# Second cross attention of a decoder megakernel: residual and normalisation of a pair moved from VectorE to ScalarE and GpSimd

## The chip, the cores and the metric

The kernel runs on one core of one Trainium2 chip. The metric is device time in microseconds of one launch, shown as the median of three runs. TensorE is called PE below, VectorE DVE, ScalarE ACT, GpSimd Pool, and SyncE (which issues the loads) SP.

## The reference

Two decoder layers with post-normalisation over 32 sequences of 56 tokens, width 128, with a context of 32 x 1500 x 128. Each layer runs attention, cross attention and a mixture of experts; the change is in the cross attention of the second layer:

```python
    def _L1_xattn_ref(x, context, ln_gamma, ln_beta, w_q, w_kv, w_out, b_out, gate):
        ...
        xn = _layernorm(x, ln_gamma, ln_beta)
        q = (xn @ w_q).reshape(B, SQ, NUM_HEADS, DIM_HEAD)
        kv = context @ w_kv
        ...
        scores = jnp.einsum('bqhd,bkhd->bhqk', q * SCALE, k)
        attn = jax.nn.softmax(scores, axis=-1)
        out = jnp.einsum('bhqk,bhkd->bqhd', attn, v).reshape(B, SQ, INNER)
        out = out @ w_out + b_out
        return out * jnp.tanh(gate[0])
...
    x = _layernorm(x + _L1_xattn_ref(x, ctx_1024, L1_xattn_ln_gamma, ...), axis=-1)
```

The outer `_layernorm` in the last line subtracts the mean over the 128 features and divides by the square root of variance plus 1e-5. It and the sum `x + ...` are what the change concerns.

## The kernel before, in words

The whole decoder is one program of phases. The phase of the change, `state_cross_phase`, works on 16 pairs of sequences (2 x 56 tokens, padded to 128 rows). For each pair there are 14 units of work (`NU`), each with 128 rows (8 queries times 16 heads) of scores against 1500 context positions. The engines' programs are written by hand as a software pipeline: `run` calls `step(i, s)` for pair `i` and slot `s` from 0 to 13; pair 0 is written out (`first`), pairs 1 to 14 are a hardware loop of 14 turns, pair 15 is written out (`end`), then comes an epilogue. Order on an engine is the order of the code; engines meet at semaphores, and every queue is in order.

In slot `s` of pair `i`:

- PE computes the scores of unit `s` (`scores`, nine matmuls of 500 columns in three pieces of three; a piece waits until the bank has been freed by DVE's `low_part` of unit `s - 2`), then one part of the value product of an older group (`values`, L2098 to L2100), then whatever the slot tables add.
- DVE inverts the sum of unit `s - 1` (`inverse`, L2226, L2228), takes the maximum of unit `s` (`maximum`, L2217 needs the first two pieces of the scores, L2221 the third), then writes the low half of the probabilities of unit `s - 1` (`low_part`, L2237, three parts).
- ACT takes the exponential of unit `s` once the maximum is there (`exponentials`, L2426, L2429, with the sum by accumulation), and writes the high half of unit `s` (`high_part`, L2445) once DVE has the inverse.
- SP issues the transposing DMA of unit `s`, and in slot 8, behind that, the load of the next pair's second context half, `load_T(i + 1, 1)` (L1807), into the only buffer `ctxT`.
- Pool prepares the next operands in 16-bit halves (`split_q`, `split_c`, `split_n`) and multiplies each context half with its scale when it has landed: `scale_c(i + 1, 1)` (L1939, 128x1500) is the last of a turn.

The output of pair `i - 1` is finished beside pair `i`. PE's output product `y` (L2133) is made in slots 7, 8 and 9 (`OUTPUT`). In slot 10 (`RESIDUAL`) DVE makes `r = gate * y + xg` between `inverse` and `maximum`, and its mean and variance (`vector_moments`, L265 and L269). Pool's `xg` (L1912) is `x` plus the gated bias; Pool adds epsilon (L274) and takes the power -1/2 (L279). In slot 11 (`NORMALISE`) DVE writes the normalised `xn` (L296) behind its `low_part`. In slot 12 (`STORE`) PE transposes `xn` (L336) behind its `values`, and ACT keeps the transposed tile (L345, L353) between its exponential and its `high_part`. In slot 13 (`LOGITS`) PE makes the router's logits (L359) from it. Pool copies `xn` back to `x_tok` (L330).

Of the kernel before, what the change touches and what calls it, by code (L numbers as in the profile page):

```python
# [28 lines left out]
PAIRS = B // 2  # L29
# [1621 lines left out]
def state_cross_phase(k):  # L1651
# [19 lines left out]
    FIRST_BANKS = (0, 1, 2, 3)  # L1671
    PROJECT, OUTPUT, RESIDUAL, NORMALISE, STORE, LOGITS = {2: 0, 3: 1, 4: 2, 5: 3}, {7: 0, 8: 1, 9: 2}, 10, 11, 12, 13
    OUTPUT_HEADS = (0, 6, 11, H1)
# [9 lines left out]
    with ExitStack() as ctx:  # L1683
# [50 lines left out]
        on = sb("on", [128, H1, 2, SP])  # L1734
        gated_bias, xg = sb("gated_bias", [128, D]), sb("xg", [128, 1, D])
        psum = ctx.enter_context(nc.psum_tensor("xa_psum", [128, 8, 512], fp32))
# [14 lines left out]
        pv_ready, on_kept = sem("pv_ready"), sem("on_kept")  # L1751
        on_zeroed, y_ready, bias_ready, xg_ready = sem("on_zeroed"), sem("y_ready"), sem("bias_ready"), sem("xg_ready")
        two_ready = sem("two_ready")
        flat_psum = psum[:, :, :].rearrange("p a b -> p (a b)")
# [107 lines left out]
        def _(pool):  # L1862
            open_sems(pool, 2, c_hi_ready, c_lo_ready, c_scaled, n_scaled, n_hi_ready, n_lo_ready, q_hi_ready, q_lo_ready)
            t.open_pool(pool)
            open_sems(pool, 1, xg_ready)

# [102 lines left out]
            def windows(i, first=False, end=False):  # L1969
                split_q(i, 1)  # L1970
                split_c(i, 1)
                split_n(i, 0, first)
                if not end:
                    scale_c(i + 1, 0)
                    split_q(i + 1, 0)
                    split_c(i + 1, 0)
                split_n(i, 1)
                if not first:
                    gated(i - 1)
                    t.pool_rstd(pool, i - 1, 0)  # L1980
                    t.pool_store(pool, i - 1, 0)
                if not end:
                    scale_c(i + 1, 1)

            for c in range(NB):
# [12 lines left out]
            gated(PAIRS - 1)  # L1998
            t.pool_rstd(pool, PAIRS - 1, 0)
            t.pool_store(pool, PAIRS - 1, 0)  # L2000

        @block.tensor
        def _(pe):
# [100 lines left out]
            def turn(i, u, r, first=False, end=False):  # L2104
# [85 lines left out]
            def epilogue():  # L2190
# [6 lines left out]
                for part in range(len(OUTPUT)):  # L2197
                    outputs(i, part)
                pe.wait_ge(t.r_ready, this(i))
                t.tensor_transpose(pe, i, 0, psum[:, 7, 128:256])  # L2200
# [6 lines left out]
        def _(dve):  # L2207
            open_sems(dve, NU, two_ready, max_ready, total_ready, rinv_ready)
            open_sems(dve, NL * NU, h2_ready)
            open_sems(dve, NR, *turn_kept.values())  # L2210
            t.open_vector(dve)

# [58 lines left out]

# [104 lines left out]
            def epilogue():  # L2376
                i = PAIRS - 1
                inverse(i, NU - 1)
                keep_turned(i, TURNED[1], 0)
                low_part(i, NU - 1)  # L2380
                keep_turned(i, TURNED[1], 1)
                keep_turned(i, TURNED[1], 2)
                residual(i)
                t.vector_normalise(dve, i, 0)
                t.vector_logits(dve, i, 0, psum[:, 7, 0:E])
# [4 lines left out]
        def _(act):  # L2390
            open_sems(act, NB, q_kept)
            open_sems(act, NU, exp_ready, bias_scaled)
            open_sems(act, 2 * NU, h1_ready)
            open_sems(act, NG, on_kept)
            t.open_scalar(act)

            def evacuate(i, g):
# [332 lines left out]
```

## Time and profile before

| | |
|---|---|
| median of 3 runs | 1885.1 us (1882.76 to 1885.45) |
| the profiled execution, its own time | 1884.88 us |
| its span, first to last instruction | 1883.0 us |
| busy over the span: PE, DVE, ACT, Pool | 1667.1, 1549.9, 1275.3, 925.5 us |
| mean granted TensorE clock | 0.96 |

A busy share is an average over phases with different limits, and PE's matmul spans overlap each other in the records (a matmul of 500 columns is shown with 0.37 us, and the next starts 0.21 us later), so the shares do not say which engine sets the pace. The phase of the change runs from about 600 to 1706 us. Within it the 14 turns of the loop repeat each other to within a few hundredths of a microsecond every 67.5 us, so that one turn read closely stands for all.

### The profile page before, as it was taken

The page shows a single profiled execution, that of the slowest core. Times are in us where ns is not written, and L with a number is a line of the kernel's source. Part 1 is how long each engine was busy: PE and PEld are TensorE (multiplying, and loading weights), DVE is VectorE, ACT ScalarE, POOL GpSimd, SP SyncE. Part 2 cuts the span into 40 slices and gives each one's busy share as a digit, 9 for nine tenths or more (in the row PEclk, how much of TensorE's full clock was granted, in tenths as well). Part 3 has the DMA queues.
Part 4 walks back from the last instruction along what each step waited for, and adds up shares of the span by engine and source line. Part 5 has one row for each costly group of instructions (what it writes and reads, how often), then busy time and mean ns, then how long its engine had stood idle before and what let it go on. Part 6 is the DMA issues. An engine that isn't in the chain of part 4 may idle for free. (4 is left out here: it accounts for less than half of the span.)

```text
span 1883.0 us, 34675 instructions
## 1 busy us (share of the span) xinstructions
PE 1667.1 (89%) x10425; PEld 1009.4 (54%) x10425; DVE 1549.9 (82%) x2885; ACT 1275.3 (68%) x2106; POOL 925.5 (49%) x723
## 2 busy tenths in 40 slices
PE   4987996889957899999999999999999999994997
PEld 2654665777733344554554554454455455454886
DVE  2765785877758999999999999999999999975887
ACT  2442332877735887887888788788788888864554
POOL 3640111363335766565665656656567465421333
PEclk9997998799978999999999999999999999997998
DMA  5203884311100898988899898898888889973231
GB/s 190 95 0 127 306 332 173 85 42 45 45 34 17 180 197 174 199 182 179 190 183 190 183 190 187 178 195 182 179 199 179 188 183 185 182 135 122 47 79 29
DMA packets 632266, 281.85 MB, mean 150 GB/s; under 512 B 601852, under 2 KB 606236, under 8 KB 631452
## 3 DMA queue, kind: packets, MB, share of 16 engines
q1 hardware_dynamic: 632204, 281.10, 64.2%
q8 instruction: 30, 0.49, 0.1%
q14 instruction: 32, 0.26, 0.0%
HBM read 129.02 MB, written 1.05 MB: 69 GB/s over the span
## 5 line engine op out<-in xcount | busy, mean ns | idle before, releaser
L2237 DVE SCALAR_TENSOR_TENSOR xa_h<-xa_psum,xa_rinv,xa_h 128x500 f16<-128x500 f32 x672 | 452.8, 730 | 1.0 <-ACT xa_h L2445 0.7
L2445 ACT ACTIVATE xa_h<-xa_psum,xa_rinv 128x1000 f16<-128x1000 f32 x448 | 371.5, 883 | 51.8 <-DVE xa_rinv L2228 51.5
L2429 ACT ACTIVATE xa_psum<-xa_psum,xa_bias,unscale_s 128x1500 f32<-128x1500 f32 x224 | 353.2, 1577 | 7.4
L2073 PE MATMUL xa_psum<-xa_c_hi,xa_q_hi 128*128 128x500 f16 x672 | 257.4, 383 | 54.5 <-DVE xa_h L2237 50.1
L2217 DVE TENSOR_REDUCE xa_psum<-xa_psum 128x1 f32<-128x1000 f32 x224 | 269.3, 1202 | 14.2 <-PE xa_psum L2075 13.4
L2098 PE MATMUL xa_psum<-xa_prT,xa_n_hi 128*128 128x512 f16 (+1 forms) x768 | 270.8, 353 | 3.6 <-issue 1.6
L2100 PE MATMUL xa_psum<-xa_prT,xa_n_lo 128*128 128x512 f16 (+1 forms) x768 | 270.6, 352 | 0.0
L2099 PE MATMUL xa_psum<-xa_prT,xa_n_hi 128*128 128x512 f16 (+1 forms) x768 | 270.6, 352 | 0.0
L2074 PE MATMUL xa_psum<-xa_c_lo,xa_q_hi 128*128 128x500 f16 x672 | 252.7, 376 | 0.0
L2075 PE MATMUL xa_psum<-xa_c_hi,xa_q_lo 128*128 128x500 f16 x672 | 252.4, 376 | 0.0
L1939 POOL TENSOR_SCALAR xa_ctxT<-xa_ctxT,scales 128x1500 f32<-128x1500 f32 x31 | 126.3, 4073 | 166.4 <-DMA xa_ctxT<-in_ctxT 166.4
L2221 DVE TENSOR_REDUCE xa_negmax<-xa_psum 128x1 f32<-128x512 f32 x224 | 154.9, 692 | 25.7
L2073 PEld LDWEIGHTS xa_psum<-xa_c_hi,xa_q_hi 128*128 128x128 f16 x672 | 65.0, 97 | 199.2 <-DVE xa_h L2237 177.7
L1463 DVE TENSOR_TENSOR moe_hid_lo<-moe_hid,moe_hid_hi 128x448 fp32r<-128x448 f32 x200 | 129.9, 675 | 34.3 <-ACT moe_hid_hi L1614 28.7
L2426 ACT ACTIVATE xa_bias<-xa_negmax,unscale_s 128x1 f32<-128x1 f32 x224 | 66.9, 299 | 134.5 <-DVE xa_negmax L2221 128.2
L1960 POOL TENSOR_SCALAR xa_ctxP<-xa_ctxP,scales 128x1536 f32<-128x1536 f32 x32 | 133.5, 4171 | 19.7 <-DMA xa_ctxP<-in_ctxP 19.7
L2098 PEld LDWEIGHTS xa_psum<-xa_prT,xa_n_hi 128*128 128x128 f16 x768 | 76.1, 99 | 92.1 <-issue 16.8
L1310 POOL TENSOR_TENSOR moe_acc<-moe_acc,moe_part 128x448 f32<-128x448 f32 x52 | 64.3, 1236 | 105.4 <-DVE moe_part L1539 53.9
L2100 PEld LDWEIGHTS xa_psum<-xa_prT,xa_n_lo 128*128 128x128 f16 x768 | 75.0, 98 | 70.2
L1610 ACT ACTIVATE moe_hid<-moe_psum,up_bias 128x448 f32<-128x448 f32 x128 | 84.2, 658 | 38.8 <-PE moe_psum L1372 34.3
L2099 PEld LDWEIGHTS xa_psum<-xa_prT,xa_n_hi 128*128 128x128 f16 x768 | 75.0, 98 | 65.2
L2075 PEld LDWEIGHTS xa_psum<-xa_c_hi,xa_q_lo 128*128 128x128 f16 x672 | 65.9, 98 | 77.5 <-issue 1.8
(328 smaller groups left out, 3630.4 us busy)
## 6 DMA issues: line engine op xcount, KB each, us to landing
ctxN<-in_ctxP SPq DMA_DIRECT2D x16, 1536.0 KB, 9.5
xa_ctxP<-in_ctxP SPq DMA_DIRECT2D x32, 768.0 KB, 4.3
ctxT<-in_ctxT SPq DMA_DIRECT2D x16, 1500.0 KB, 6.4
xa_ctxT<-in_ctxT SPq DMA_DIRECT2D x32, 750.0 KB, 4.7
moe_spread<-weight_rows SPq DMA_DIRECT2D x16, 1024.0 KB, 8.4
xa_prT<-xa_h SPq DMA_TRANSPOSE x192, 5.5
up<-in_F_up SPq DMA_DIRECT2D x1, 2048.0 KB, 7.7
down<-in_F_down SPq DMA_DIRECT2D x1, 2048.0 KB, 11.8
```

What stands on the lines that cost most here:

```text
L1960: pool.tensor_scalar(ctxP[:, :], ctxP[:, :], k.scales[:, 0:1], None, ALU.mult).then_inc(n_scaled, 1)
L2073: nc.tensor.matmul(out, qh, c_hi[:, b, a:z], start=True, stop=False)
L2074: nc.tensor.matmul(out, qh, c_lo[:, b, a:z], start=False, stop=False)
L2075: done = nc.tensor.matmul(out, ql, c_hi[:, b, a:z], start=False, stop=True)
L2098: nc.tensor.matmul(out, nh, ph, start=(kt == 0), stop=False)
L2099: nc.tensor.matmul(out, nh, pl, start=False, stop=False)
L2100: done = nc.tensor.matmul(out, nl, ph, start=False, stop=(kt == KT - 1))
L2217: nc.vector.tensor_reduce(psum[:, bank + 1, W:W + 1], psum[:, bank:bank + 2, 0:W], AX.XY, ALU.max)\
L2221: nc.vector.tensor_reduce(negmax[:, s % 2, :], flat_psum[:, top:top + 512], AX.X, ALU.max, negate=True)\
L2237: nc.vector.scalar_tensor_tensor(low, psum[:, bank + a:bank + z, 0:W], rinv[:, s % 2, :], high, ALU.mult, ALU.subtract).then_inc(h2_ready, 1)
L2429: nc.scalar.activation(psum[:, bank:bank + 3, 0:W], psum[:, bank:bank + 3, 0:W], ACT.Exp, bias=bias[:, s % 2, :], scale=k.unscale_s[:, :], ...
L2445: nc.scalar.activation(h[:, H_SLOT[s], 0, a * W:z * W].rearrange("p (a c) -> p a c", c=W), psum[:, bank + a:bank + z, 0:W], ACT.Identity, ...
```

## The change

VectorE no longer has the residual, the moments and the normalisation of a pair. ACT and Pool make them, in another arithmetic: the sum of `xg` (ACT, slot 7, `sum_x`) and the sum of the gated `y` (ACT, slot 9, `gate`, which also writes the gated `y` to the new tile `yg`) come by accumulation; Pool adds `r = yg + xg` and makes minus the mean (`residual`); ACT squares `r` minus the mean with the sum by accumulation (slot 11, `square`); Pool makes variance plus epsilon, the power, `xn`, and its copy (`normalise`). `gated` is earlier in Pool's turn. PE, where it waited for `r_ready` before it overwrote the bank of `y`, waits for `yg_ready`. The two moments differ from those of `bn_stats` in rounding alone.

```diff
@@ gpsimd @@
             def gated(i):
                 pool.wait_ge(bias_ready, 1)
                 pool.wait_ge(t.r_ready, last(i))
+                pool.sem_inc(gating, 1)
+                pool.wait_ge(x_sum_ready, last(i))
                 pool.tensor_tensor(xg[:, :, :], k.x_tok[:, bass.ds(i, 1), :], gated_bias[:, :].unsqueeze(1), ALU.add)\
                     .then_inc(xg_ready, 1)
+
+            def residual(i):
+
+                pool.wait_ge(yg_ready, this(i))
...
+                pool.tensor_tensor(t.r[:, :, :], yg[:, :, :], xg[:, :, :], ALU.add).then_inc(t.r_ready, 1)
+                pool.wait_ge(x_sum_ready, this(i))
+                pool.sem_inc(gating, 1)
+                pool.tensor_scalar(neg_mean[:, :], y_sum[:, :], x_sum[:, :], -1.0 / D, ALU.add, ALU.mult)\
+                    .then_inc(neg_mean_ready, 1)
+
+            def normalise(i):
+
+                pool.wait_ge(squares_ready, this(i))
...
+                pool.tensor_scalar(t.var_eps[:, 0, :], squares[:, :], 1.0 / D, k.eps[:, :], ALU.mult, ALU.add)\
+                    .then_inc(t.var_eps_ready, 1)
...
+                pool.tensor_tensor(t.rstd[:, 0, :], t.var_eps[:, 0, :], k.minus_half[:, :], ALU.pow).then_inc(t.rstd_ready, 1)
...
+                pool.tensor_scalar(t.xn[:, 0, :], t.r[:, 0, :], neg_mean[:, :], t.rstd[:, 0, :], ALU.add, ALU.mult)\
+                    .then_inc(t.xn_ready, 1)
+                t.pool_store(pool, i, 0)
...
                 split_n(i, 0, first)
+                if not first:
+                    gated(i - 1)
                 if not end:
                     scale_c(i + 1, 0)
                     split_q(i + 1, 0)
                     split_c(i + 1, 0)
                 split_n(i, 1)
                 if not first:
-                    gated(i - 1)
-                    t.pool_rstd(pool, i - 1, 0)
-                    t.pool_store(pool, i - 1, 0)
+                    residual(i - 1)
                 if not end:
                     scale_c(i + 1, 1)
+                if not first:
+                    normalise(i - 1)
@@ tensor @@
                 if u == TURNED[0] and r == 1 and not first:
-                    pe.wait_ge(t.r_ready, this(i - 1))
+                    pe.wait_ge(yg_ready, this(i - 1))
@@ vector @@
-            def residual(i):
-
-                dve.wait_ge(y_ready, this(i))
-                dve.wait_ge(xg_ready, this(i))
-                nc.vector.scalar_tensor_tensor(t.r[:, 0, :], psum[:, 7, 0:128], k.gate_tanh[:, :], xg[:, 0, :],
-                                               ALU.mult, ALU.add).then_inc(t.r_ready, 1)
-                t.vector_moments(dve, i, 0)
...
-                if s == RESIDUAL and not first:
-                    residual(i - 1)
...
-                if not first:
-                    if s == NORMALISE:
-                        t.vector_normalise(dve, i - 1, 0)
@@ scalar @@
+            def sum_x(i):
...
+                nc.scalar.activation(yg[:, 0, :], xg[:, 0, :], ACT.Identity, accum_out=x_sum[:, :]).then_inc(x_sum_ready, 1)
+
+            def gate(i):
+
+                act.wait_ge(y_ready, this(i))
+                act.wait_ge(x_sum_ready, this(i))
+                nc.scalar.activation(yg[:, 0, :], psum[:, 7, 0:128], ACT.Identity, scale=k.gate_tanh[:, :],
+                                     accum_out=y_sum[:, :]).then_inc(yg_ready, 1)
+
+            def square(i):
+
+                act.wait_ge(t.r_ready, this(i))
+                act.wait_ge(neg_mean_ready, this(i))
+                act.wait_ge(t.var_eps_ready, last(i))
+                nc.scalar.activation(yg[:, 0, :], t.r[:, 0, :], ACT.Square, bias=neg_mean[:, :],
+                                     accum_out=squares[:, :]).then_inc(squares_ready, 1)
...
             def step(i, s, first=False, end=False):
                 exponentials(i, s)
+                if s == min(OUTPUT) and not first:
+                    sum_x(i - 1)
+                if s == max(OUTPUT) and not first:
+                    gate(i - 1)
+                if s == SQUARES and not first:
+                    square(i - 1)
                 if s == STORE and not first:
                     t.scalar_store(act, i - 1, 0, psum[:, 7, 128:256])
```

Where the instructions stand. First DVE, slot 10 of a loop turn, before the change; line 2217 is the first half of `maximum`:

```order
704 L2228 RECIPROCAL xa_rinv<-xa_total 128x1
705 L2249 REGISTER_ALU
706 L2251 SCALAR_TENSOR_TENSOR xa_r<-xa_psum,gate_tanh,xa_xg 128x128
707 L265 BN_STATS xa_moments<-xa_r 128x6
708 L269 BN_AGGR xa_mean_var<-xa_moments 128x2
709 L2216 REGISTER_ALU
710 L2217 TENSOR_REDUCE xa_psum<-xa_psum 128x1
```

With the change nothing stands between the two in that slot (`maximum` is line 2260 there, the reciprocal 2271):

```order
704 L2271 RECIPROCAL xa_rinv<-xa_total 128x1
705 L2259 REGISTER_ALU
706 L2260 TENSOR_REDUCE xa_psum<-xa_psum 128x1
```

Three instructions before a `maximum` are gone from DVE, and the one of slot 11 (L296) too.

Second Pool, the end of a loop turn, before the change; the branch is the loop's end:

```order
339 L1967 TENSOR_TENSOR xa_n_lo<-xa_ctxP,xa_n_hi 128x1536
340 L1912 ISA
341 L1912 TENSOR_TENSOR xa_xg<-x_tok,xa_gated_bias 128x128
342 L274 TENSOR_TENSOR xa_var_eps<-xa_mean_var,eps 128x1
343 L279 TENSOR_TENSOR xa_rstd<-xa_var_eps,minus_half 128x1
344 L330 COPY x_tok<-xa_xn 128x128
345 L1937 REGISTER_ALU
346 L1939 TENSOR_SCALAR xa_ctxT<-xa_ctxT,scales 128x1500
347 L1995 REGISTER_ALU
348 L1995 COMPARE_AND_BRANCH
```

The same place with the change:

```order
341 L2008 TENSOR_TENSOR xa_n_lo<-xa_ctxP,xa_n_hi 128x1536
342 L1928 TENSOR_TENSOR xa_r<-xa_yg,xa_xg 128x128
343 L1931 TENSOR_SCALAR xa_neg_mean<-xa_y_sum,xa_x_sum 128x1
344 L1978 REGISTER_ALU
345 L1980 TENSOR_SCALAR xa_ctxT<-xa_ctxT,scales 128x1500
346 L1940 TENSOR_SCALAR xa_var_eps<-xa_squares,eps 128x1
347 L1945 TENSOR_TENSOR xa_rstd<-xa_var_eps,minus_half 128x1
348 L1952 TENSOR_SCALAR xa_xn<-xa_r,xa_neg_mean,xa_rstd 128x128
349 L330 COPY x_tok<-xa_xn 128x128
350 L2038 REGISTER_ALU
```

The scaling of the context (128x1500) stood behind the pair's tail; it now stands ahead of variance, power and `xn`.

Third ACT in slots 12 and 13 of the changed kernel, where the order itself did not change (L345 waits for PE's transposition of `xn`):

```order
621 L2480 ACTIVATE xa_psum,xa_rs<-xa_psum,xa_bias,unscale_s 128x3x500
622 L345 ACTIVATE xa_xnT<-xa_psum 128x128
623 L353 ISA
624 L353 ACTIVATE x_feat<-xa_psum 128x112
625 L2496 ACTIVATE xa_h<-xa_psum,xa_rinv 128x1000
```

The store still stands between exponential and high half, so ACT too waits there if `xn` is late.

## Rows read from the trace of the kernel before

**Rows 1.** Windows: busy time (and count) of each engine, clock, DMA share, GB/s

```profile
core 0: us, PE busy (x) PEld busy (x) DVE busy (x) ACT busy (x) POOL busy (x), PEclk, DMA share, GB/s
1285.00:1350.00 65.00, 62.14 (x391) 32.48 (x388) 59.97 (x105) 53.99 (x82) 38.94 (x21) 1.00 0.90 189
```

**Rows 2.** Timeline of DVE: start, duration, line; idle before and its releaser

```profile
1253.54 1.21 DVE L2217 TENSOR_REDUCE xa_psum<-xa_psum 128x1 f32<-128x1000 f32 x1 [0.48 <-PE xa_psum L2075]
...
1258.02 0.35 DVE L2251 SCALAR_TENSOR_TENSOR xa_r<-xa_psum,gate_tanh,xa_xg 128x128 f32<-128x128 f32 x1
...
1258.85 0.18 DVE L269 BATCH_NORM_AGGREGATE xa_mean_var<-xa_moments 128x2 f32<-128x6 f32 x1 [0.15 <-DVE xa_moments L265]
1259.08 1.21 DVE L2217 TENSOR_REDUCE xa_psum<-xa_psum 128x1 f32<-128x1000 f32 x1
...
1267.96 0.34 DVE L296 TENSOR_SCALAR xa_xn<-xa_r,xa_mean_var,xa_rstd 128x128 f32<-128x128 f32 x1
...
1273.49 1.21 DVE L2217 TENSOR_REDUCE xa_psum<-xa_psum 128x1 f32<-128x1000 f32 x1
...
1703.17 0.35 DVE L296 TENSOR_SCALAR xa_xn<-xa_r,xa_mean_var,xa_rstd 128x128 f32<-128x128 f32 x1 [0.93 <-POOL xa_rstd L279]
```

**Rows 3.** Timeline of PE: sixth score matmuls, starts after a wait, the transposition

```profile
1253.13 0.37 PE L2075 MATMUL xa_psum<-xa_c_hi,xa_q_lo 128*128 128x500 f16 x1
...
1258.09 0.37 PE L2075 MATMUL xa_psum<-xa_c_hi,xa_q_lo 128*128 128x500 f16 x1
...
1261.81 0.38 PE L2073 MATMUL xa_psum<-xa_c_hi,xa_q_hi 128*128 128x500 f16 x1 [0.32 <-DVE xa_h L2237]
...
1270.69 0.27 PE L336 MATMUL xa_psum<-ident,xa_xn 128*128 128x128 f32 x1
1271.82 0.39 PE L2073 MATMUL xa_psum<-xa_c_hi,xa_q_hi 128*128 128x500 f16 x1 [0.85 <-DVE xa_h L2237]
...
1272.89 0.37 PE L2075 MATMUL xa_psum<-xa_c_hi,xa_q_lo 128*128 128x500 f16 x1
...
1703.66 0.42 PE L336 MATMUL xa_psum<-ident,xa_xn 128*128 128x128 f32 x1 [2.47 <-DVE xa_xn L296]
```

**Rows 4.** Instructions of line 2251: count, durations, first and last start

```profile
L2251 DVE SCALAR_TENSOR_TENSOR xa_r<-xa_psum,gate_tanh,xa_xg x16: 350/351/352, 717.7 to 1701.2; 128x128 f32<-128x128 f32 x16
```

**Rows 5.** Timeline of ACT in slots 9 to 12

```profile
1258.11 1.66 ACT L2445 ACTIVATE xa_h<-xa_psum,xa_rinv 128x1000 f16<-128x1000 f32 x2 [0.48 <-DVE xa_rinv L2228]
...
1267.97 0.19 ACT L2429 ACTIVATION_READ_ACCUMULATOR xa_psum<-xa_psum,xa_bias,unscale_s 128x1 f32 x1
...
1273.08 0.27 ACT L345 ACTIVATE xa_xnT<-xa_psum 128x128 f32<-128x128 f32 x1
```

**Rows 6.** Timeline of Pool

```profile
1233.99 4.07 POOL L1939 TENSOR_SCALAR xa_ctxT<-xa_ctxT,scales 128x1500 f32<-128x1500 f32 x1 [11.08 <-DMA xa_ctxT<-in_ctxT]
...
1259.11 0.19 POOL L274 TENSOR_TENSOR xa_var_eps<-xa_mean_var,eps 128x1 f32<-128x1 f32 x1 [2.66 <-DVE xa_mean_var L269]
1259.38 0.57 POOL L279 TENSOR_TENSOR xa_rstd<-xa_var_eps,minus_half 128x1 f32<-128x1 f32 x1
...
1268.74 4.08 POOL L1939 TENSOR_SCALAR xa_ctxT<-xa_ctxT,scales 128x1500 f32<-128x1500 f32 x1
```

**Rows 7.** Timeline of SP: issues of the two context loads of a turn

```profile
1229.06 0.35 SPq L1807 DMA_DIRECT2D xa_ctxT<-in_ctxT  x1
...
1261.66 0.34 SPq L1807 DMA_DIRECT2D xa_ctxT<-in_ctxT  x1
```

**Rows 8.** Groups of Pool's instructions, whole span: busy us, mean ns

```profile
L1287 POOL TENSOR_SCALAR key_query<-key_query,scales 128x512 f32<-128x512 f32 x4 | 9.6, 2392 | 0.0
...
L1912 POOL TENSOR_TENSOR xa_xg<-x_tok,xa_gated_bias 128x128 f32<-128x128 f32 x16 | 7.3, 458 | 0.0
...
L1875 POOL TENSOR_SCALAR ss_spread_inner<-ss_mean_var 128x4 f32<-128x4 f32 x4 | 2.9, 720 | 12.6 <-DVE ss_mean_var L2320 12.5
...
L1900 POOL TENSOR_SCALAR xa_gated_bias<-bout_row1x,gate_tanh 128x128 f32<-128x128 f32 x1 | 0.6, 618 | 0.0
```

More of the change, by code:

```diff
@@ L1671, in state_cross_phase @@
     FIRST_BANKS = (0, 1, 2, 3)
-    PROJECT, OUTPUT, RESIDUAL, NORMALISE, STORE, LOGITS = {2: 0, 3: 1, 4: 2, 5: 3}, {7: 0, 8: 1, 9: 2}, 10, 11, 12, 13
+    PROJECT, OUTPUT, SQUARES, STORE, LOGITS = {2: 0, 3: 1, 4: 2, 5: 3}, {7: 0, 8: 1, 9: 2}, 11, 12, 13
     OUTPUT_HEADS = (0, 6, 11, H1)
@@ L1734, in state_cross_phase @@
         on = sb("on", [128, H1, 2, SP])
-        gated_bias, xg = sb("gated_bias", [128, D]), sb("xg", [128, 1, D])
+        gated_bias, xg, yg = sb("gated_bias", [128, D]), sb("xg", [128, 1, D]), sb("yg", [128, 1, D])
+        y_sum, x_sum, neg_mean, squares = (sb(n, [128, 1]) for n in ("y_sum", "x_sum", "neg_mean", "squares"))
         psum = ctx.enter_context(nc.psum_tensor("xa_psum", [128, 8, 512], fp32))
@@ L1752, in state_cross_phase @@
         on_zeroed, y_ready, bias_ready, xg_ready = sem("on_zeroed"), sem("y_ready"), sem("bias_ready"), sem("xg_ready")
+        yg_ready, x_sum_ready, sum_ready = sem("yg_ready"), sem("x_sum_ready"), sem("sum_ready")
+        neg_mean_ready, squares_ready, gating = sem("neg_mean_ready"), sem("squares_ready"), sem("gating")
         two_ready = sem("two_ready")
@@ L1864, in _ @@
             t.open_pool(pool)
+            open_sems(pool, 1, t.r_ready, t.xn_ready, neg_mean_ready)
             open_sems(pool, 1, xg_ready)
@@ L1911, in gated @@
                 pool.wait_ge(t.r_ready, last(i))
+                pool.sem_inc(gating, 1)
+                pool.wait_ge(x_sum_ready, last(i))
                 pool.tensor_tensor(xg[:, :, :], k.x_tok[:, bass.ds(i, 1), :], gated_bias[:, :].unsqueeze(1), ALU.add)\
                     .then_inc(xg_ready, 1)
+            def residual(i):
+                pool.wait_ge(yg_ready, this(i))
+                pool.sem_inc(gating, 1)
+                pool.wait_ge(squares_ready, last(i))
+                pool.sem_inc(gating, 1)
+                pool.wait_ge(t.xn_ready, last(i))
+                pool.tensor_tensor(t.r[:, :, :], yg[:, :, :], xg[:, :, :], ALU.add).then_inc(t.r_ready, 1)
+                pool.wait_ge(x_sum_ready, this(i))
+                pool.sem_inc(gating, 1)
+                pool.tensor_scalar(neg_mean[:, :], y_sum[:, :], x_sum[:, :], -1.0 / D, ALU.add, ALU.mult)\
+                    .then_inc(neg_mean_ready, 1)
+            def normalise(i):
+                pool.wait_ge(squares_ready, this(i))
+                pool.sem_inc(gating, 1)
+                pool.wait_ge(t.rstd_ready, last(i))
+                pool.sem_inc(gating, 1)
+                pool.tensor_scalar(t.var_eps[:, 0, :], squares[:, :], 1.0 / D, k.eps[:, :], ALU.mult, ALU.add)\
+                    .then_inc(t.var_eps_ready, 1)
+                pool.wait_ge(t.var_eps_ready, this(i))
+                pool.sem_inc(gating, 1)
+                pool.wait_ge(t.xn_ready, last(i))
+                pool.tensor_tensor(t.rstd[:, 0, :], t.var_eps[:, 0, :], k.minus_half[:, :], ALU.pow).then_inc(t.rstd_ready, 1)
+                pool.wait_ge(t.rstd_ready, this(i))
+                pool.sem_inc(gating, 1)
+                pool.wait_ge(t.xnT_ready, last(i))
+                pool.sem_inc(gating, 1)
+                pool.wait_ge(t.tok_stored, last(i))
+                pool.sem_inc(gating, 1)
+                pool.tensor_scalar(t.xn[:, 0, :], t.r[:, 0, :], neg_mean[:, :], t.rstd[:, 0, :], ALU.add, ALU.mult)\
+                    .then_inc(t.xn_ready, 1)
+                t.pool_store(pool, i, 0)
             def split_q(i, b):
@@ L1998, in _ @@
             gated(PAIRS - 1)
-            t.pool_rstd(pool, PAIRS - 1, 0)
-            t.pool_store(pool, PAIRS - 1, 0)
+            residual(PAIRS - 1)
+            normalise(PAIRS - 1)
         @block.tensor
@@ L2198, in epilogue @@
                     outputs(i, part)
-                pe.wait_ge(t.r_ready, this(i))
+                pe.wait_ge(yg_ready, this(i))
                 t.tensor_transpose(pe, i, 0, psum[:, 7, 128:256])
@@ L2210, in _ @@
             open_sems(dve, NR, *turn_kept.values())
-            t.open_vector(dve)
+            open_sems(dve, 1, t.logits_kept)
             def maximum(i, s):
@@ L2382, in epilogue @@
                 keep_turned(i, TURNED[1], 2)
-                residual(i)
-                t.vector_normalise(dve, i, 0)
                 t.vector_logits(dve, i, 0, psum[:, 7, 0:E])
@@ L2394, in _ @@
             open_sems(act, NG, on_kept)
+            open_sems(act, 1, x_sum_ready, yg_ready, squares_ready)
             t.open_scalar(act)
+            def sum_x(i):
+                act.wait_ge(xg_ready, this(i))
+                act.wait_ge(squares_ready, last(i))
+                act.wait_ge(neg_mean_ready, last(i))
+                nc.scalar.activation(yg[:, 0, :], xg[:, 0, :], ACT.Identity, accum_out=x_sum[:, :]).then_inc(x_sum_ready, 1)
[10 more added lines that the diff above has]
+                                     accum_out=squares[:, :]).then_inc(squares_ready, 1)
             def evacuate(i, g):
@@ L2515, in epilogue @@
                         evacuate(*at)
+                sum_x(PAIRS - 1)
+                gate(PAIRS - 1)
+                square(PAIRS - 1)
                 t.scalar_store(act, PAIRS - 1, 0, psum[:, 7, 128:256])
```

## The prediction, made blind

> **What bounds the kernel now.** Windows first. A stretch of about one loop turn has PE busy 62.1 of 65 us, DVE 60.0, ACT 54.0, Pool 38.9, at full clock [rows 1]. PE and DVE are both near full, so the shares decide nothing; the order of waits inside a turn does. The timelines give it, read at one turn; its 14 copies start 67.5 us apart.
>
> In most slots DVE sets the pace: inverse, maximum, low half, with PE waiting for the low half to free a bank, as in slot 11 at 1261.81 after 0.32 us idle and in slot 13 at 1271.82 after 0.85 us [rows 3]. Slots 8 to 10 are different, since PE also makes the output product there: the maximum of slot 9 starts at 1253.54 after 0.48 us idle, released by PE [rows 2]. Its sixth score matmul started at 1253.13 [rows 3], so a maximum can start 0.41 us after the sixth matmul's start. That rule prices everything below.
>
> **What goes from DVE.** In slot 10 the residual, the statistics and the aggregation stand between 1258.02 and 1259.08, when the maximum starts [rows 2]: 1.06 us on DVE's path. But PE's sixth matmul of that slot started at 1258.09 [rows 3], so without them the maximum waits for PE until 1258.50. The gain is 0.58 us, not 1.06. It survives slot 11 nearly whole: PE had 0.32 us of idle there and would start at 1261.49; its sixth matmul at 1.07 more (1271.82 to 1272.89 is the same distance [rows 3]) allows the maximum at 1262.97, about where DVE, 0.58 us early, asks for it. I take 0.55. The `xn` of slot 11, at 1267.96 for 0.34 us [rows 2], ends at 1268.30, 0.14 us after ACT's accumulator read of the same slot (1267.97 + 0.19 = 1268.16 [rows 5]), which the next inverse needs anyway: removing it is worth 0.1 us at most, and I take nothing.
>
> **What ACT gets.** Three activations of 128x128 with a sum: 0.27 us for such a tile and 0.19 for the accumulator read [rows 5], about 0.45 each. They follow the exponentials of slots 7, 9 and 11, where ACT otherwise waits for DVE's inverse, 0.48 us in slot 9 [rows 5]. That wait hides them; if it were gone they would cost 0.45 us each, up to 1.4 per turn. Dearer ones (0.65) would still push only a high half, which DVE needs after the whole maximum. Cost taken: nothing. The gated `y` is there at about 1258.0, and the turned-tile matmuls of PE that wait for it come after slot 10's values, so that wait costs nothing either.
>
> **What Pool gets, and where it lands.** Here I expect the time to go. Before, Pool made variance and power at 1259.11 and 1259.38 (0.19 and 0.57 us), waited for DVE's `xn`, and only then scaled the context, at 1268.74 for 4.08 us [rows 6]. Now `scale_c` stands ahead of variance, power and `xn`. It can't run early: its data's load is issued by SP in slot 8, behind a transposing DMA, at 1261.66 [rows 7], and nothing of the change moves slot 8. Landing: the other load of the turn was issued at 1229.06 [rows 7] and Pool, which was waiting for it, started at 1233.99 [rows 6], 4.93 us later. I take 4.85: `scale_c` runs from 1266.5 to 1270.6. The squares are there by about 1268.1, so Pool's queue, not ACT, holds the tail back.
>
> Then the three operations on Pool. Variance: a tensor_scalar of one column, not in this trace; below by the add of 0.19 us [rows 6], above by the 128x4 with two operations, 0.72 us [rows 8]; I take 0.4, between them, as it is a quarter as wide. Power: 0.57 [rows 6]. `xn`: a tensor_scalar of 128x128 with two operations; below by the add of that size, 0.46, nearer by the one with one operation, 0.62 [rows 8]; above by 2.39 us for 512 columns [rows 8], which scaled by size and doubled for two operations gives 1.2; I take 0.8. Two gaps of 0.08 (1259.11 + 0.19 to 1259.38 [rows 6]). Sum N = 0.4 + 0.57 + 0.8 + 0.16 = 1.93, bounds 1.38 and 2.65. So `xn` is there at 1270.57 + 1.93 = 1272.50, where it was at 1268.30.
>
> PE transposed at 1270.69, without a wait [rows 3], and would be there by 1270.15 now. It must wait for `xn`. After a late `xn`, in the epilogue, the matmul started 0.14 us after its end (1703.17 + 0.35 [rows 2] to 1703.66 [rows 3]). So transposition at 1272.64, the scores of slot 13 queued behind it at about 1272.8, their sixth matmul 1.07 later, the maximum at 1274.28. It was 1273.49 [rows 2]. The 0.55 us of slot 10 are lost and 0.79 us more. ACT, which waits in slot 12 for the transposed tile before its high half, has it at 1272.9 and is done before DVE's low half asks; the logits come later than both. Nothing gives the time back: PE and DVE shift alike.
>
> In sentences of its own: the Trainium skill, page GPSIMD Engine Reference, section Engine selection, says that one-input elementwise work on Pool runs at roughly line rate, and its cycle accounting gives about 1.03 cycles an element for it. By that, `xn` would be some 0.3 us (an estimate from that page) and a pair would lose about 0.1 us. Here the trace disagrees: 1500 columns of a one-input multiplication took 4.07 us [rows 6], 2.7 ns each, so I stay with the rows.
>
> **The sum.** 14 turns hold `scale_c` ahead of the tail: 14 x 0.79 = +11.1 us. Pair 15's steps have no such load and keep the gain: -0.5. The epilogue is serial: from the residual's start at 1701.2 [rows 4] to `xn`'s end at 1703.52 [rows 2] was 2.3 us. Now: gate 0.45, `r` 0.46, minus mean 0.4, square 0.45, variance 0.4, power 0.57, `xn` 0.8, and six hand-overs of 0.08 make 4.0: +1.7. Together +12.3. The profiled execution took 1884.9 (span 1883.0), the median is 1885.1; the forecast is 1897.
>
> Bounds: with N = 1.38 a turn loses 0.24, with cheap Pool work the epilogue +1.1: +4.0, 1889. With N = 2.65, 1.51 a turn and +3 at the end: +23.6, 1908.
>
> **The rivals.** Faster (0.11): Pool's tail does not hold PE. Point of decision: a turn wins if the maximum of slot 13 starts before 1273.49, so `xn` must be there by 1271.7. This needs the load landed 0.8 us sooner than its twin, or N below 1.14, under my lower bound. For it: the gain of slot 10 is certain, and PE has 0.85 us of slack before slot 13. If the tail were wholly hidden: 14 x -0.55 - 0.5 + 1.7 = -6.5, 1878.5.
>
> About no change (0.09): the Pool operations cost what the cheapest rows say, or the page's rule holds, and the loss of a turn is 0.0 to 0.25 us. That gives 1885 to 1889. Against it: no tensor_scalar in the rows is as cheap as an add.
>
> Slower by another way (0.05): PE's idle stretch of 2.5 us a turn makes the granted clock fall from 2.4 to 1.2 GHz. In the rows it stayed at 1.00 with 0.85 us of idle per turn [rows 1, 3]. If slot 13's nine score matmuls then ran at half speed, 9 x 0.21 = 1.9 us a turn, +27 more: 1924. Slower by ACT, with its three extras on the path, would be 14 x 1.4 less the gain: 1897 also, told apart by where DVE waits. The forecast itself has 0.75.
>
> **Numbers.** Range 1884 to 1908: the forecast with its bounds and the no-change case; the faster case and the clock stay out. Within 0.2% (3.8 us, about what a measurement of this kernel can tell): 0.10, faster 0.11, slower 0.79.
>
> **What the profile after would show.** No DVE instruction between reciprocal and maximum in slot 10, the maximum starting 0.4 us after PE's sixth matmul. `scale_c` of the second half starting on a DMA wait, about 4.9 us after its issue, ending some 2 us before `xn`. PE idle over 2 us before L336, released by Pool's `xn`, once a turn; DVE idle 1.4 us before slot 13's maximum, released by PE. A loop turn of 68.3 us. I am wrong if L336 has no wait, if Pool runs the small operations in under 1.2 us together, if the load lands before 1265.5 in this turn's time, or if ACT's idle before its bias is used up in slots 7, 9 or 11.

## The result, and the profile after

Before: 1883.4 us median of 6 runs (1881.3 to 1885.5). After: 1901.1 us median of 6 runs (1896.9 to 1907.8). The ratio is 1.0097 with a 95% interval of 1.0078 to 1.0116: slower by some 17.6 us, where 12 were forecast. The profiled execution of after is the slowest of its six, 1907.8 us with a span of 1905.9, against 1884.9 and 1883.0 before; what follows must explain 22.9 us in this one execution and 17.6 in the median, and the two are not the same.

First the page of after, its busy times and two of its groups (busy us, mean ns, then idle time just before and what ended it):

```profile
PE 1671.2 (88%) x10425; PEld 1018.8 (53%) x10425; DVE 1536.6 (81%) x2821; ACT 1289.8 (68%) x2202; POOL 944.9 (50%) x771
...
L2260 DVE TENSOR_REDUCE xa_psum<-xa_psum 128x1 f32<-128x1000 f32 x224 | 269.3, 1202 | 47.7 <-PE xa_psum L2118 47.6
...
L1980 POOL TENSOR_SCALAR xa_ctxT<-xa_ctxT,scales 128x1500 f32<-128x1500 f32 x31 | 126.1, 4067 | 267.9 <-DMA xa_ctxT<-in_ctxT 267.9
```

The maximum (L2260, the L2217 of before) sat idle for 14.2 us in the whole program before, nearly all of it for PE; now it is 47.7. The waits between the start of the first pair's loop turn and the last one's, in after, grouped by who waited and for what (total us, count, longest):

```profile
DVE xa_psum L2260 <- PE xa_psum L2118: 43.0, 59, 3.3
...
PE xa_psum L336 <- POOL xa_xn L1952: 33.8, 14, 3.0
```

Fourteen waits of PE for Pool's `xn` are one per turn, 2.4 us each (1.9 to 3.0). Before, the transposition started in the loop without a wait [rows 3]. The timeline of Pool in the turn that the prediction followed, now 1265 to 1282 (start, duration, line, operation; idle before it and its releaser):

```profile
1266.24 0.45 POOL L1928 TENSOR_TENSOR xa_r<-xa_yg,xa_xg 128x128 f32<-128x128 f32 x1 [2.22 <-ACT xa_yg L2437]
1266.67 0.27 POOL L1931 TENSOR_SCALAR xa_neg_mean<-xa_y_sum,xa_x_sum 128x1 f32<-128x1 f32 x1
1274.38 4.07 POOL L1980 TENSOR_SCALAR xa_ctxT<-xa_ctxT,scales 128x1500 f32<-128x1500 f32 x1 [7.44 <-DMA xa_ctxT<-in_ctxT]
1278.44 0.26 POOL L1940 TENSOR_SCALAR xa_var_eps<-xa_squares,eps 128x1 f32<-128x1 f32 x1
1278.89 0.57 POOL L1945 TENSOR_TENSOR xa_rstd<-xa_var_eps,minus_half 128x1 f32<-128x1 f32 x1 [0.18 <-POOL xa_var_eps L1940]
1279.87 0.44 POOL L1952 TENSOR_SCALAR xa_xn<-xa_r,xa_neg_mean,xa_rstd 128x128 f32<-128x128 f32 x1 [0.41 <-POOL xa_rstd L1945]
```

Pool stands idle for 7.44 us for the load, with the tail queued behind the scaling, and the tail's input long there: ACT's accumulator read of the squares started at 1275.76 and took 0.19. The load's issue on SP:

```profile
1265.67 3.66 SPq L1833 DMA_TRANSPOSE xa_prT<-xa_h  x1
1269.67 0.34 SPq L1810 DMA_DIRECT2D xa_ctxT<-in_ctxT  x1
```

From 1269.67 to 1274.38 are 4.71 us. PE and DVE in the same turn, PE first:

```profile
1277.94 0.33 PE L2143 MATMUL xa_psum<-xa_prT,xa_n_lo 128*128 128x384 f16 x1
1280.45 0.30 PE L336 MATMUL xa_psum<-ident,xa_xn 128*128 128x128 f32 x1 [2.19 <-POOL xa_xn L1952]
1280.59 0.37 PE L2116 MATMUL xa_psum<-xa_c_hi,xa_q_hi 128*128 128x500 f16 x1
1281.64 0.37 PE L2118 MATMUL xa_psum<-xa_c_hi,xa_q_lo 128*128 128x500 f16 x1
```

```profile
1265.84 0.16 DVE L2271 RECIPROCAL xa_rinv<-xa_total 128x1 f32<-128x1 f32 x1
1266.49 1.21 DVE L2260 TENSOR_REDUCE xa_psum<-xa_psum 128x1 f32<-128x1000 f32 x1 [0.49 <-PE xa_psum L2118]
...
1280.78 0.16 DVE L2271 RECIPROCAL xa_rinv<-xa_total 128x1 f32<-128x1 f32 x1
1282.06 1.21 DVE L2260 TENSOR_REDUCE xa_psum<-xa_psum 128x1 f32<-128x1000 f32 x1 [1.11 <-PE xa_psum L2118]
```

In slot 10 (first two rows) nothing is left between reciprocal and maximum but 0.49 us of waiting for PE: the time from slot 9's maximum to this one went from 5.53 to 4.96 us, 0.57 less. In slot 13 (last two) DVE waits 1.11 us for PE, whose scores stand behind the transposition: the time from slot 12's maximum to slot 13's went from 4.39 us to 5.25 at the least.

That is what was forecast. The lengths of the 14 loop turns (start of the maximum of slot 0 to the next one's) show what was not:

| | turns, us | sum |
|---|---|---|
| before | 67.5 each | 945.4 |
| after, forecast | 68.3 each | 956.5 |
| after, 7 turns | 67.85 to 68.45, mean 68.12 | 476.9 |
| after, the other 7 | 69.32 to 70.39, mean 69.83 | 488.8 |

The long ones are 1.7 us longer than the short ones. Two things are in that. Their load came later: PE's wait for `xn` has a mean of 2.7 us in them and 2.15 in the short ones, 0.5 us of the 1.7. In each of the seven short turns the length is 65.97 or 65.98 us plus that wait, so a wait longer by some time makes the turn longer by the same time. The long turns hold 1.0 to 1.4 us beyond that sum, 1.2 on average. These 1.2 are here, in the windows of one of them, with the granted clock behind the busy times of PE, PEld, DVE, ACT and Pool:

```profile
1345.00:1348.00 3.00, 1.43 (x9) 0.65 (x7) 2.87 (x5) 2.13 (x4) 2.82 (x3) 1.00 1.03 196
1348.00:1350.00 2.00, 0.93 (x3) 0.55 (x4) 0.93 (x3) 1.18 (x5) 0.81 (x3) 0.61 0.95 186
1350.00:1352.00 2.00, 2.00 (x6) 0.73 (x5) 0.00 (x0) 1.54 (x2) 0.00 (x0) 0.54 0.78 310
1352.00:1354.00 2.00, 2.00 (x14) 1.30 (x13) 1.84 (x3) 0.00 (x0) 1.11 (x2) 1.00 0.00 0
```

PE is busy without a break up to 1346.43 (the 1.43 us of the first window), then idle for 2.64, and comes back to a clock at half, 1.2 GHz instead of 2.4, until six of the nine score matmuls are through. Its timeline there:

```profile
1349.07 0.45 PE L336 MATMUL xa_psum<-ident,xa_xn 128*128 128x128 f32 x1 [2.64 <-POOL xa_xn L1952]
1349.31 0.63 PE L2116 MATMUL xa_psum<-xa_c_hi,xa_q_hi 128*128 128x500 f16 x1
1349.73 0.62 PE L2117 MATMUL xa_psum<-xa_c_lo,xa_q_hi 128*128 128x500 f16 x1
...
1351.39 0.61 PE L2118 MATMUL xa_psum<-xa_c_hi,xa_q_lo 128*128 128x500 f16 x1
```

0.61 instead of 0.37, and a maximum that starts 2.97 us after the transposition instead of 1.61. Such a fall is in each of the seven long turns and in no short one. The moment differs: in this turn the clock is at half 0.63 us before PE works again, in others only when PE has worked for up to 1.1 us. So this execution's loop holds 7 x 0.6 + 7 x 2.3 = +20.3 us. Pair 15 and the epilogue (last slot-0 maximum to the start of PE's transposition of `xn`) went from 87.65 to 89.15, +1.5. Together +21.8 of the 22.9; the rest lies behind that transposition, in phases that the change leaves alone.

### The profile page after: what moved, and what is told of

The parts are those of the page before. It is cut to its first block and busy times, and to the rows that moved or that the text cites. A ratio compares the mean times of both kernels' runs of the same rounds, so it can differ in the third digit from the quotient of the medians.

```text
span 1905.9 us, 34885 instructions
## 1 busy us (share of the span) xinstructions
PE 1671.2 (88%) x10425; PEld 1018.8 (53%) x10425; DVE 1536.6 (81%) x2821; ACT 1289.8 (68%) x2202; POOL 944.9 (50%) x771
## 5 line engine op out<-in xcount | busy, mean ns | idle before, releaser
L2260 DVE TENSOR_REDUCE xa_psum<-xa_psum 128x1 f32<-128x1000 f32 x224 | 269.3, 1202 | 47.7 <-PE xa_psum L2118 47.6
```

The costliest lines, as they stand in the source:

```text
L2260: nc.vector.tensor_reduce(psum[:, bank + 1, W:W + 1], psum[:, bank:bank + 2, 0:W], AX.XY, ALU.max)\
```

## The experiments

Theory A, after the result: Pool's order. The tail stands behind a scaling that waits for a load, `xn` is late for PE, and the late `xn` costs a turn directly (0.6 to 0.8 us) and, when the clock falls in PE's idle stretch, over a microsecond more. Theory B: the operations added to ACT and Pool, or the removed ones of DVE, are dear wherever they stand. Theory C: the lost time is all clock. The times before in each pair below are of the same chip in the same hours.

**e1_tail_first.** One call of Pool's order is moved, so that the tail stands ahead of the load-bound scaling:

```diff
                 if not first:
                     residual(i - 1)
+                    normalise(i - 1)
...
                 scale_c(i + 1, 1)
-                if not first:
-                    normalise(i - 1)
```

> The changed kernel with Pool's normalise put back ahead of scale_c of the second context half; ACT's and DVE's parts are as changed. Theory (the tail is late because it stands behind scale_c, which waits for its load): xn is ready about 1.9 us after the squares, before PE reaches its transposition or at most a few tenths after, PE's wait before L336 goes from 2.2 us and more to under 0.3 us, no turn shows half clock, a loop turn takes 67.0 us (67.5 before, less the 0.57 us of slot 10), and the time is 14 x 0.57 + 0.3 = 8.3 below before, plus 1.7 for the epilogue: about 1877, ratio 0.9965. Rival A (Pool's arithmetic itself is too slow, wherever it stands): L336 still waits over 1 us, 1890 or more. Rival B (ACT's three extra activations are on the path): slots 8, 10 and 12 get longer by some 0.4 us each, over 1895.

Measured: 1879.2 us, median of 12 runs, against 1884.2 before: ratio 0.9972 [0.9961, 0.9983]. All arithmetic of the change is in it, and it is faster than before (1877 was expected). Pool and PE in its timeline:

```profile
1266.31 0.27 POOL L1940 TENSOR_SCALAR xa_var_eps<-xa_squares,eps 128x1 f32<-128x1 f32 x1 [9.32 <-ACT xa_yg L2444]
1267.74 0.45 POOL L1952 TENSOR_SCALAR xa_xn<-xa_r,xa_neg_mean,xa_rstd 128x128 f32<-128x128 f32 x1 [0.41 <-POOL xa_rstd L1945]
1268.63 4.08 POOL L1980 TENSOR_SCALAR xa_ctxT<-xa_ctxT,scales 128x1500 f32<-128x1500 f32 x1
```

```profile
1268.33 0.30 PE L336 MATMUL xa_psum<-ident,xa_xn 128*128 128x128 f32 x1
1269.26 0.38 PE L2115 MATMUL xa_psum<-xa_c_hi,xa_q_hi 128*128 128x500 f16 x1 [0.63 <-DVE xa_h L2279]
```

The tail runs before the load has landed, `xn` is there at 1268.2, and PE transposes without a wait. The 14 turns last 66.98 us on average (673.17 to 1610.83), all at full clock. Measured from maximum to maximum, this turn differs from before in two slots alone: 0.58 us less up to slot 10's and 0.12 more from slot 13's to the next slot 0's, of which more below; every other slot is within 0.01. So neither ACT's three activations nor the missing `xn` of DVE shows in the turn. Theory B falls; the scaling, put behind the tail, starts without any wait and is late for nobody.

**e3_load_slot7.** Pool's order stays as in after, and the load is issued a slot earlier:

```diff
-                if s == 8 and not end:
+                if s == 7 and not end:
                     load_T(i + 1, 1)
```

> The changed kernel with one number different: SP issues the load of the second context half in slot 7, not 8, and Pool's order is as changed (scale_c ahead of the tail). Theory: the load lands 4.9 us sooner, scale_c ends at about 1265.7 of the turn shown, before the squares are there, so the tail is as early as with the order undone: about 1877, turns of 67.0 us, full clock. Rival (it is the place in the queue as such, not the landing): no better than 1897. If the earlier load delays the transposing DMAs behind it, values of PE start late in slots 11 and 12, and the gain is smaller by that wait.

Measured: 1879.4 us, median of 12, ratio 0.9976 [0.9964, 0.9987]; turns of 66.98 us. The issue on SP, then Pool:

```profile
1252.18 0.34 SPq L1810 DMA_DIRECT2D xa_ctxT<-in_ctxT  x1
```

```profile
1257.39 4.07 POOL L1980 TENSOR_SCALAR xa_ctxT<-xa_ctxT,scales 128x1500 f32<-128x1500 f32 x1 [3.05 <-DMA xa_ctxT<-in_ctxT]
...
1263.66 0.27 POOL L1940 TENSOR_SCALAR xa_var_eps<-xa_squares,eps 128x1 f32<-128x1 f32 x1 [2.20 <-ACT xa_yg L2445]
```

Now the tail waits for ACT and no longer for the load. Two edits that share nothing but the tail no longer waiting for the load give the same turn within 0.01 us: the place is found.

**e4_before_swapped.** The kernel before, with all its work on DVE, and only Pool's order spoiled in the same way:

```diff
-                    t.pool_rstd(pool, i - 1, 0)
-                    t.pool_store(pool, i - 1, 0)
...
                 scale_c(i + 1, 1)
+                if not first:
+                    t.pool_rstd(pool, i - 1, 0)
+                    t.pool_store(pool, i - 1, 0)
```

> The kernel before, with nothing moved between engines, only scale_c of the second half put ahead of Pool's variance and power (pool_rstd) and store. Theory: the power is ready only when scale_c has ended, 4.07 us after a landing at 1266.4 of the turn shown: 1271.3 with 0.85 us of variance and power; DVE stands in its queue with xn from 1267.95 on, so it stalls some 3.3 us and everything behind it: +3.3 x 14 = +46, 1930. This is worse than the change (0.6 to 2.8 us a turn), since there only PE, with 0.85 us of slack, stands and waits. Rival (the order matters little and the change's loss is in its arithmetic): within 5 us of before.

Measured: 1945.9 us, median of 4, ratio 1.0328 [1.0311, 1.0346]: +62, the largest number of the study, with none of the change in it. In its timeline Pool first, then DVE, where the normalisation stands in the middle of the queue and holds every maximum behind it:

```profile
1300.78 4.07 POOL L1939 TENSOR_SCALAR xa_ctxT<-xa_ctxT,scales 128x1500 f32<-128x1500 f32 x1 [9.68 <-DMA xa_ctxT<-in_ctxT]
1305.08 0.57 POOL L279 TENSOR_TENSOR xa_rstd<-xa_var_eps,minus_half 128x1 f32<-128x1 f32 x1
```

```profile
1305.68 0.34 DVE L296 TENSOR_SCALAR xa_xn<-xa_r,xa_mean_var,xa_rstd 128x128 f32<-128x128 f32 x1 [3.02 <-POOL xa_rstd L279]
```

The slot takes 8.1 to 8.6 us instead of 5.0, the 3.3 that I expected; but a turn is 4.4 us longer (the 14 take 61.4 more), and the other 1.1 us, 15 in all, I had not in my number. Windows there (the clock is the first figure behind the five busy times):

```profile
1306.00:1310.00 4.00, 0.78 (x4) 0.35 (x4) 3.84 (x8) 2.75 (x4) 0.29 (x1) 1.00 0.96 266
1310.00:1314.00 4.00, 4.00 (x16) 1.93 (x15) 3.69 (x9) 3.57 (x8) 1.51 (x2) 0.62 0.06 23
```

PE is busy 0.78 of 4 us, and the clock is at half behind it; such a fall is in all 14 turns. The 1.1 us lie in the two slots behind the stall, in which the clock is at half (0.9 to 2.2 us by turn); all slots ahead of it last as long as before. So a direct loss and one with the clock are here also. PE's idle time around the transposition is 1.49 us ahead of it and 2.25 behind it in this turn, more together than in after, and here no turn was spared.

**e2_filled and e5_filled_loop.** To part the clock from the late `xn`: after, with matmuls whose result nobody reads put into PE's wait, 18 of 256 columns, in a bank's unused half. e2 has them in all of pairs 1 to 15, e5 leaves them out in pair 15. The edit of e5:

```diff
+                    for x in range(0 if end else FILL):
+                        nc.tensor.matmul(psum[:, 7, 256:512], k.kq_hi[:, 0, :],
+                                         k.kq_hi[:, 0:2, :], start=True, stop=True)
                     t.tensor_transpose(pe, i - 1, 0, psum[:, 7, 128:256])
```

> The changed kernel with 18 matmuls of 256 columns of a constant tile, whose result nobody reads, on PE in slot 12 just before its wait for xn (1.9 us of work in a stretch in which PE is idle for 2.2 us and more). Theory (two separate losses: the late xn itself, about 0.6 us a turn against before, and half clock after the idle stretch, about 1.3 to 2.3 us in those turns in which it falls): all 14 turns look like the fast ones of the profile after, 67.9 to 68.5 us, no half clock in the loop, 14 x 0.6 + 1.5 = 10 above before, about +1 for pair 15, where nothing waits and the filling is in the way: 1893 to 1895, some 6 us below the changed kernel. Rival (the slow turns are slow because of DMA or Pool, and the clock is only a mark of them): the spread of turns stays, time as with the change, 1901.

> As the filled kernel before, but the 18 filling matmuls stand only in the turns in which scale_c is ahead of the tail (pairs 1 to 14), not in pair 15, where they cost 1.0 us. Compared on one chip with the changed kernel itself. Theory (the idle stretch of PE costs a clock fall in some turns, a loss of its own): no turn at half clock, turns of 67.8 to 68.7 us by how late the load lands, 14 x 0.7 + 1.5 = 11 to 13 above before, and below the changed kernel by 1.7 us for each of its turns at half clock. Rival (the clock falls are harmless here): equal to the changed kernel within 0.1%.

Measured: e2 1900.0, median of 6, ratio 1.0084 [1.0068, 1.0101]; e5 1899.2, median of 6, ratio 1.0067 [1.0053, 1.0081]. PE's timeline in e5:

```profile
1277.64 2.13 PE L2204 MATMUL xa_psum<-kq_hi 128*128 128x256 f16 x18
1280.33 0.33 PE L336 MATMUL xa_psum<-ident,xa_xn 128*128 128x128 f32 x1 [0.56 <-POOL xa_xn L1953]
```

PE is idle 0.56 us instead of 2.2, no loop turn of either shows a clock below 1.00, and none is longer than 69.0 us: e5's 14 last 956.5 us together, 68.3 each, which is the forecast's sum. Theory C falls, since most of the loss stays. But e2 had been expected at 1893 to 1895, 6 us under after, as I had taken seven long turns for typical; it is only 1 us under after's median. Its own loop, +10.4 us on before, is as expected; its last stretch is 2.8 us longer than before, since the filling is in the way of pair 15, and in its profile the loop starts 2 us later than before's (in all the profiles here it starts between 667.8 and 673.2 us). That asked for after a second time.

**e6_after_again.** After, unchanged, on the same chip as e5.

> The changed kernel once more, unaltered, for the comparison on one chip and a second profile. Theory: ratio 1.0097 as measured; the turns fall in two groups again, 67.8 to 68.6 us at full clock and 69 to 70.5 at half clock, in another number than the 7 of the first profile, since which turns fall is not fixed by the program; the time of the profiled execution moves by some 1.7 us for each. Rival (the slow turns belong to fixed pairs): the same turns are slow.

Measured: 1902.2 us, median of 4, ratio 1.0093 [1.0077, 1.0109], against e5's 1899.2. Its profiled execution is its fastest, 1897.5, and there only one turn of 14 has the half clock. The windows in that turn:

```profile
1612.00:1618.00 6.00, 3.62 (x21) 1.71 (x19) 5.54 (x11) 4.87 (x9) 5.24 (x5) 1.00 1.04 210
1618.00:1622.00 4.00, 4.00 (x16) 2.12 (x17) 2.44 (x6) 2.28 (x5) 1.16 (x2) 0.66 0.62 204
```

Its other 13 turns have a mean of 68.3 us, each 65.95 or 65.96 plus PE's wait; the 14 are 957.5 together, +12.1 on before. It is the last turn that has the half clock, and six others that had it in the first profile have not. So how many turns the clock spoils is not fixed by the program: 7 in one execution of after, 1 in another, with nearly the same idle before the transposition (37.5 us in all before L336, 38.2 in after's). Nor is it a matter of the idle's length alone: in after's profile the clock fell behind an idle of 2.12 us in one turn and not behind 2.48 in another, and e6 has one of 2.88 without a fall. The two profiled executions are the slowest (1907.8) and the fastest but one (1897.5) of ten; their loops are 8.2 us apart, and six more falls of 1.2 make 7.2 of that.

**e7_epilogue_dve.** e1, and the last pair's residual, statistics and normalisation made by DVE again, in the epilogue alone. Not shown in the cut: ACT's three activations of the last pair go, and PE waits for `r_ready` there.

```diff
 # DVE, epilogue
+                residual(i)
+                t.vector_normalise(dve, i, 0)
 # Pool, epilogue
-            residual(PAIRS - 1)
-            normalise(PAIRS - 1)
+            t.pool_rstd(pool, PAIRS - 1, 0)
+            t.pool_store(pool, PAIRS - 1, 0)
 # DVE, start of the phase
+            open_sems(dve, PAIRS, t.moments_ready, t.mean_var_ready)
```

> The kernel with Pool's tail ahead of scale_c, and in the epilogue, where the chain is serial and DVE idle, the last pair's residual, moments and normalisation on DVE as before the change. Theory: from the residual's start to xn's end 2.3 us again instead of 4.2, so 1.9 us below that kernel's profile and about 7.5 below before: ratio 0.9961, the fastest of all. Rival (the epilogue is hidden by loads or table loads of the next phase): no difference to the kernel with the order undone.

Measured: 1876.4 us, median of 6, ratio 0.9953 [0.9939, 0.9967], the fastest version of the study. The last stretch went from e1's 89.2 to 87.3, as expected. Its timeline of DVE in the epilogue:

```profile
1688.62 0.35 DVE L2294 SCALAR_TENSOR_TENSOR xa_r<-xa_psum,gate_tanh,xa_xg 128x128 f32<-128x128 f32 x1 [14.54 <-PE xa_psum L2175]
...
1690.57 0.34 DVE L296 TENSOR_SCALAR xa_xn<-xa_r,xa_mean_var,xa_rstd 128x128 f32<-128x128 f32 x1 [0.94 <-POOL xa_rstd L279]
```

2.3 us from the residual's start to `xn`'s end, as before, where ACT and Pool take 4.2 (from the start of ACT's `gate`). But its loop turns were 66.86 us, and not e1's 66.98, and no edit of e7 is in the loop. In e1 the reciprocal of slot 0 stood so on DVE (e1's timeline):

```profile
1275.23 0.16 DVE L2270 RECIPROCAL xa_rinv<-xa_total 128x1 f32<-128x1 f32 x1
1275.46 0.69 DVE L2285 COPY xa_prT<-xa_psum 128x1024 f16<-128x1024 f16 x1
```

and in e7's:

```profile
1268.81 0.17 DVE L2271 RECIPROCAL xa_rinv<-xa_total 128x1 f32<-128x1 f32 x1
1268.91 0.69 DVE L2286 COPY xa_prT<-xa_psum 128x1024 f16<-128x1024 f16 x1
```

From one start to the next 0.23 us there, 0.10 here. Before had 0.11.

**e8_two_more and e9_tail_first_again.** e8 is e1 with only the last edit of e7: two semaphores more, raised once at the start of the phase on DVE, at 549.7 us, over 700 us ahead of these rows, and waited for by nobody. e9 is e1 again, on e8's chip.

> The kernel with Pool's tail ahead of scale_c, and two more semaphore increments in DVE's program ahead of its first work (of two semaphores nobody waits for); nothing else. In the profile of that kernel DVE starts the copy of slot 0 0.23 us after its reciprocal starts, in the one with DVE's epilogue put back 0.10 us, although both have the same loop; the loop turns were 66.99 and 66.86 us. Theory (where the loop's instructions lie in DVE's program decides, since the only other difference of the two is DVE's code ahead of and behind the loop): with the two increments ahead of it the gap is 0.10 us and the turn 66.86 us, 14 x 0.13 = 1.8 us below. Rival (it is the epilogue's code behind the loop, or chance of one execution): the gap stays 0.23 and the turn 66.99.

> The kernel with Pool's tail ahead of scale_c, unaltered, beside the one before on one chip. Theory: turns of 66.99 us again and a gap of 0.23 us, ratio 0.9972 again, since both belong to the program and not to an execution. Rival: turns of 66.86 us.

Measured: e8 1876.3 (6 runs), ratio 0.9961 [0.9939, 0.9982], turns of 66.86; e9 1877.9 (11 runs), ratio 0.9970 [0.9960, 0.9980], turns of 66.98. In e8 the copy again starts 0.10 us behind the reciprocal:

```profile
1273.94 0.17 DVE L2271 RECIPROCAL xa_rinv<-xa_total 128x1 f32<-128x1 f32 x1
1274.04 0.69 DVE L2286 COPY xa_prT<-xa_psum 128x1024 f16<-128x1024 f16 x1
```

So 0.13 us a turn hangs on these two increments: with them 66.86 us in e7 and 66.85 in e8, without them 66.98 in e1 and 66.97 in e9. Whether it is through the place of the loop's code behind them, as I think, or in another way, no run shows. The medians, 1.7 us apart, fit 14 x 0.13, but their intervals overlap. The change took four such increments off DVE at this place, and in after, e2, e3, e5 and e6 too the slot around this copy lasts 5.14 us where it lasted 5.02 before.

## Why the prediction was right, and where it was off

**What goes from DVE.** Right. Not 1.06 us but 0.57 is gained in slot 10 (0.58 and then 0.55 forecast), since PE's sixth matmul then releases the maximum, 0.49 us after DVE is free [rows 2, 3 for before]. e1's turns, 0.55 us shorter than before, show that it reaches the turn: 0.58, less 0.12 in the slot of the copy, and at most 0.01 less in each of the other slots, 0.09 together. The going of `xn` from slot 11 is worth nothing, as taken.

**What ACT gets.** Right. The extras took 0.30, 0.36 and 0.39 us and 0.19 for each sum's read, a little more than the 0.45 taken, and e1 keeps them all without a slot getting longer for them.

**Where the work lands on Pool.** Right, and this carried the sign. `scale_c` waited for the load in the turn followed, 4.71 us after issue (4.85 taken); the three operations behind it ended 1.86 us after its end (N = 1.93). The size came out by two misses that nearly cancel: variance 0.26, power 0.57 and `xn` 0.44 are 1.27 us against 1.77 taken, but the two hand-overs were 0.18 and 0.41 against 0.08 each. That N came out is therefore luck: under 1.2 us of work I had said I would be wrong, and it was 1.27. The tensor_scalar of 128x128 cost what an add of that size does; the 0.8, set between a row of 0.62 and 1.2 scaled from 512 columns, was too dear. A slip beside the sum: an `xn` of 0.3 us alone gives, by the prediction's own terms, a loss of 0.29 us a turn and not 0.1; the forecast's sum does not use it.

**The wait of PE.** Right: 14 waits at L336, 2.4 us on average. At full clock a turn lost 0.6 us in one profile, 0.8 in another (later loads), 0.8 with the clock held up (e5), against 0.79. But 0.13 of each belongs to the slot of the copy, which the prediction did not have; without it the losses would be 0.5 to 0.7, so that the match with 0.79 is in part luck. The late `xn` itself, seen against e1, costs 1.1 to 1.3 us a turn.

**Pair 15 and the epilogue.** -0.5 + 1.7 = +1.2 forecast, +1.5 measured; from the start of ACT's `gate` to `xn`'s end 4.2 us (4.0 forecast), and e7 gives 1.9 of it back.

**The clock.** This is the step that failed: the median is 5 us over the forecast, and on e5's chip, where it can be told apart, some 3 us are the clock's share. It stood as a rival of 0.05 that would spoil every turn for +27 us, on the ground that the clock had stayed at 1.00 with 0.85 us idle per turn [rows 1, 3]. That row says nothing of an idle stretch three times as long. In truth the clock fell in some turns, 7 and 1 of 14 in the two profiles, for about 1.2 us each (1.9 forecast; in the turn shown six of the nine matmuls ran at half speed). It should have been a term with a share, not a rival with all or nothing. The Trainium skill, page TensorE: Matmul & The Clock Gate, section Part 1: The HAM clock gate, also ties the clock to how busy PE was shortly before; the runs agree in kind, e4 above all (0.78 busy of 4 us, a fall in every turn). The same part says that the watching goes on free of the kernel, so that the place of a change varies from run to run. The moments of the eight falls in the two profiles of after agree in kind: they come from 2.0 to 4.1 us after PE fell idle, so the idle stretch alone does not set them. That would give 7 falls and 1, but no run here shifts the one against the other.

So for the median: on e5's chip the loop without clock falls accounts for +11.1 and the last stretch for +1.6, 12.8 of the 13.4 us that e5 is slower than before. After is another 3.0 us slower there by the medians, which I put down to the clock; the two intervals of the ratio just overlap, so its size is known only roughly. The forecast's 12.3 was the part without the clock, and that part was right within 1 us, with the two strokes of luck named above in it.

What stays open: how many falls an execution typically has and why the same program has 1 or 7, and why two increments ahead of the loop matter in one place of it.

## What to carry to other kernels

Work that moves to another engine moves into that engine's queue; look for what in that queue waits for a transfer, and put the short work that others need ahead of it. Here one call, moved by a few lines, turns +0.97% into -0.3%. With the serial epilogue kept on the engine that does it in fewest hand-overs it is -0.5%, of which the two increments are about as large a part as the epilogue (1.8 and 1.9 us by the profiles). An operation freed on the busiest engine is worth only the time until the next engine's release. And a wait on PE can have a second price in its clock, as the waits of 2.1 to 3.0 us had here in 1 to 7 of 14 turns; it should be in the sum with a share of the turns.

## What the hardware showed that I had not expected

- PE, busy without a break and then idle for 1.9 to 3.0 us once a turn, lost its clock (2.4 to 1.2 GHz) in some turns (idle 2.1 to 3.0) and not in others (1.9 to 2.9) of one program, now during the idle time, now up to 1.3 us after it; a 128x500 f16 matmul then took 0.61 to 0.63 us instead of 0.37. Matmuls without use, filling the wait, kept it at 2.4.
- On Pool a result handed to the next operation of Pool itself cost 0.18 us of idle behind a 0.26 us operation, and 0.41 behind the power of 0.57 us.
- Two more semaphore increments at the start of the phase on DVE shortened every turn of the loop behind them by 0.13 us, all between one reciprocal and the copy behind it.
